# A selective state-space loop on one core: where the softplus mask lies, when the rows of C and x are projected, and when the step product is made

## The reference

```python
zxbcdt = hidden_states @ W_in.T
z, x, Bm, Cm, dtl = jnp.split(zxbcdt, splits, axis=-1)
delta = jax.nn.softplus(dtl @ W_dt.T + b_dt + b_dt)
x = repeat(x); x = jax.nn.silu(causal_conv4(x, conv_w) + conv_b)
def step(state, inp):                       # over 64 positions
    dA = jnp.exp(dlt[..., None] * A_g)      # 16 states a channel
    du = (dlt * u)
    state = dA * state + du[..., None] * Bs[:, :, None, :]
    y = jnp.einsum('bgdn,bgn->bgd', state, Cs)
    return (state, y)
y = ys + x * D_param
y = y * jax.nn.silu(z)
return y @ W_out.T
```

## Time and profile before

| what | value |
|---|---|
| median of three runs | 927.2 us |
| the profiled execution's own time | 926.82 us |
| span from its first to its last instruction | 924.9 us |
| state-space loop, first scan to end of the last | 41.5 to 273.8 us |
| DVE busy over the span | 548.1 us (59%) |
| ACT busy | 434.1 us (47%) |
| POOL busy | 302.3 us (33%) |
| PE busy | 818.7 us (89%) |

### The profile page before, as it was taken

The page is one execution under the profiler, slowest core; times in us unless marked ns, Lnnn a source line. Parts: engine busy times, 40 slices in busy tenths (PEclk is TensorE's granted clock), DMA queues, the critical chain, the costliest instruction groups (busy, mean ns, idle before and its releaser), DMA issues.

```text
span 924.9 us, 12509 instructions
## 1 busy us (share of the span) xinstructions
PE 818.7 (89%) x5082; PEld 501.8 (54%) x5082; DVE 548.1 (59%) x666; ACT 434.1 (47%) x650; POOL 302.3 (33%) x147
## 2 busy tenths in 40 slices
PE   6687797977999889999999899997989799989976
PEld 2232333322445456566666676666677566667754
DVE  3799989899994232333433452437872534464686
ACT  3764666635524555555545312233554222232475
POOL 0089999899870000000001010102009990000000
PEclk9889999899999999999999999998989999999999
DMA  9666666776994100000000031415000000000001
GB/s 301 176 172 172 185 166 172 181 182 181 249 264 157 47 1 1 1 1 1 1 1 25 27 103 57 176 44 226 2 3 1 1 1 1 1 1 1 1 1 46
DMA packets 26377, 77.02 MB, mean 83 GB/s; under 512 B 3569, under 2 KB 10481, under 8 KB 25073
## 3 DMA queue, kind: packets, MB, share of 16 engines
q1 hardware_dynamic: 25552, 74.13, 27.8%
q0 software_dynamic: 768, 2.10, 0.6%
HBM read 68.75 MB, written 7.08 MB: 82 GB/s over the span
## 4 chain that ended last, share of the span: by engine, by line
PE 54%; DVE 13%; DMA 11%; ACT 10%; POOL 6%; issue 5%; SPq 0%; POOLq 0%; DVEq 0%; ACTq 0%
PE ps L1268 11%; PE ps L1184 9%; DMA region_b<-m_rows 5%; DMA region_c<-m_rows 4%; PE ps L1231 4%; PE ps L1367 4%; PE ps L1393 4%; POOL region_c L464 3%; PE ps L1256 3%; PE ps L1189 2%; POOL region_b L464 2%; DVE region_c L1827 2%; PE ps L1073 2%; PE ps L1025 2%; PE ps L1158 2%
## 5 line engine op out<-in xcount | busy, mean ns | idle before, releaser
L464 POOL TENSOR_TENSOR region_c<-region_c,region_b 128x1024 f32<-128x1024 f32 x42 | 101.1, 2415 | 51.6 <-DMA region_b<-m_rows 45.5
L1073 PE MATMUL ps<-region_c,ident 128*128 128x512 f32 x168 | 90.7, 669 | 18.9 <-POOL region_c L464 12.1
L1827 DVE TENSOR_TENSOR_SCAN region_c<-region_c,ps 128x1024 f32<-128x1024 f32 x43 | 97.8, 2283 | 2.0 <-ACT ps L635 0.8
L485 POOL DMA_INDIRECT f_in<-xn,f_row x8 | 8.0, 996 | 275.3 <-DVE f_row L1938 273.5
L1268 PE MATMUL ps<-region_c 128*128 128x256 f32 x384 | 90.4, 381 | 0.1
L1268 PEld LDWEIGHTS ps<-region_c 128*128 128x128 f32 x384 | 72.2, 190 | 24.8 <-issue 16.3
L1904 DVE COPY region_b<-ps 128x512 f32<-128x512 f32 x32 | 21.6, 689 | 84.9 <-PE ps L1242 84.8
L1822 DVE TENSOR_TENSOR ps<-ps,region_c 128x1024 f32<-128x1024 f32 x52 | 63.2, 1215 | 8.7 <-PE ps L1061 8.5
L1073 PEld LDWEIGHTS ps<-region_c,ident 128*128 128x128 f32 x168 | 33.7, 209 | 58.5 <-issue 34.5
L1184 PE MATMUL ps<-xnT,region_a 128*128 128x512 f32 x128 | 61.5, 602 | 0.8 <-ACT region_c L703 0.8
L1184 PE MATMUL ps<-xnT,region_c 128*128 128x512 f32 x128 | 58.6, 594 | 0.7 <-ACT region_c L731 0.7
(11 more groups left out here) (246 smaller groups left out, 1640.8 us busy)
## 6 DMA issues: line engine op xcount, KB each, us to landing
region_b<-m_rows SPq DMA_DIRECT2D x43, 512.0 KB, 5.1
region_c<-m_rows SPq DMA_DIRECT2D x21, 512.0 KB, 4.9
xn<-m_brows SPq DMA_DIRECT2D x12, 512.0 KB, 4.4
region_a<-in_x_wo SPq DMA_DIRECT2D x2, 2048.0 KB, 11.5
m_rows<-region_b SPq DMA_DIRECT2D x4, 512.0 KB, 5.7
region_a<-in_x_wq SPq DMA_DIRECT2D x8, 256.0 KB, 7.2
region_b<-in_f_fc SPq DMA_DIRECT2D x1, 2048.0 KB, 7.9
region_b<-in_f_proj SPq DMA_DIRECT2D x1, 2048.0 KB, 13.2
```

Of the source, the lines that this page charges most:

```text
L464: pool.tensor_tensor(m_hc[u % 3], m_h[u % 3], m_cb[u % 3], ALU.mult).then_inc(sem("m_hc"), 1)
L1073: last = pe.matmul(ps[:, 4 + c, :], ident[:, :], m_hc[u % 3][:, c * HALF:c * HALF + HALF], start=(n == 0), stop=(n == DST - 1))
L1827: dve.tensor_tensor_scan(m_h[u % 3], m_da[u % 3].rearrange("p b t -> p (b t)"), inputs(u), 0.0, ALU.mult, ALU.add).then_inc(sem("m_scan"), 1)
```

## The change

1. The mask of the selection is written to PSUM pair 6, the pair into which the projections of C, x, z and the later convolutions go, and no longer to SBUF. So it has to lie between the C rows (and x rows) and the convolution: the convolution moves from n = 11 to n = 12 on PE and waits for the selection (`m_sel`), its copy on ACT from n = 12 to n = 13.
2. The C rows are projected at n = 2 and 3, not 3 and 4 (the first half ahead of `add_state`), and copied by ACT at n = 4, not 6. x is projected at n = 5 and 6, not 7 and 8, and copied at n = 7 and 8, not 9 and 10. The mask follows at n = 8, not 7.
3. The step product has a buffer for each block: `m_du` is a list, with the context's `ctxT` as block 1's buffer and the C rows' `m_rowsT` as block 3's. POOL makes it one step sooner, ahead of the state product of n = 13, directly behind the sum that gives delta. The load of `ctxT` moves from the start of the program to step 50.
4. On ACT the decay of a block's first step is issued ahead of the Silu `channels` of the same block, and not behind the two Silus.

The diff, whole but for its context:

```diff
-        m_du = view("C", 56, [TOK])
+        m_du = [view("C", 56, [TOK]), ctxT[:, :], view("C", 56, [TOK]), m_rowsT]
 # SP
-            load(ctxT[:, :], io["ctxT"], "ld_x0")
...
                     if n == 2:
                         sp.wait_ge(sem("m_delta"), NK)
                         sp.wait_ge(sem("m_u"), NK)
+                        sp.wait_ge(sem("m_pd"), len(SHARED) * (NK - 2))
+                        sp.wait_ge(sem("m_dbu"), own_products(DST * (NK - 2) - 1))
+                        load(ctxT[:, :], io["ctxT"], "ld_x0")
 # POOL
             def step_inputs(k):
                 pool.wait_ge(sem("m_u"), k + 1)
                 pool.wait_ge(sem("m_delta"), k + 1)
-                pool.wait_ge(sem("m_pd"), len(SHARED) * k)
-                pool.wait_ge(sem("m_dbu"), own_products(DST * k - 1))
-                pool.tensor_tensor(m_du, m_delta[k % 2].rearrange("p b t -> p (b t)"), m_u[:, k, :], ALU.mult)\
+                if k == 2:
+                    pool.wait_ge(sem("m_pd"), len(SHARED))
+                    pool.wait_ge(sem("m_dbu"), own_products(DST - 1))
+                if k == 3:
+                    pool.wait_ge(sem("st_rows"), 16 * NK)
+                pool.tensor_tensor(m_du[k], m_delta[k % 2].rearrange("p b t -> p (b t)"), m_u[:, k, :], ALU.mult)\
                     .then_inc(sem("m_du"), 1)
...
-                if n == DST - 2 and k < NK - 1:
+                if n == DST - 3 and k < NK - 1:
                     step_inputs(k + 1)
 # ACT
             def step_below(k):
-                act.activation(m_below, m_e, ACT.Relu, scale=-1.0, bias=thr_col).then_inc(sem("m_below"), 1)
+                act.wait_ge(sem("m_cT"), k + 1)
+                if k == 2:
+                    act.wait_ge(sem("m_xs"), 2)
+                act.activation(pair(6), m_e, ACT.Relu, scale=-1.0, bias=thr_col).then_inc(sem("m_below"), 1)
...
-            for u in range(NK * DST):
+            def decay(u):
                 k, n = u // DST, u % DST
                 if n == 0:
                     act.wait_ge(sem("m_delta"), k + 1)
...
+            for u in range(NK * DST):
+                k, n = u // DST, u % DST
+                if n or not k:
+                    decay(u)
...
-                    if n == 6:
+                    if n == 4:
                         c_rows(k + 1)
-                    if n == 7:
+                    if n in (7, 8) and k == 1:
+                        lags(1, (2 * n - 14, 2 * n - 13))
+                    if n == 8:
                         step_below(k + 1)
-                    if n in (9, 10) and k == 1:
-                        lags(1, (2 * n - 18, 2 * n - 17))
-                    if n == 12:
+                    if n == 13:
                         convolved(k + 1)
                     if n == DST - 1:
+                        decay(u + 1)
                         channels(k + 1)
 # PE
+                if n == 2 and k < NK - 1:
+                    pe.wait_ge(sem("m_ax"), k + 2)
+                    columns("C", k + 1, (0,))
                 if u >= 2:
                     add_state(u - 2)
...
-                    if n in (3, 4):
-                        pe.wait_ge(sem("m_ax"), k + 2)
-                        columns("C", k + 1, (n - 3,))
-                    if n in (7, 8) and k == 1:
+                    if n == 3:
+                        columns("C", k + 1, (1,))
+                    if n in (5, 6) and k == 1:
                         pe.wait_ge(sem("m_cT"), 3)
-                        columns("x", 1, (n - 7,))
-                    if n == 11:
-                        if k != 1:
-                            pe.wait_ge(sem("m_cT"), k + 2)
+                        columns("x", 1, (n - 5,))
+                    if n == 12:
+                        pe.wait_ge(sem("m_sel"), k + 1)
                         convolve(k + 1)
 # DVE: the selection reads pair(6), the products m_du[k]
-                dve.copy_predicated(m_ln, m_below.bitcast(mybir.dt.uint32), m_poly).then_inc(sem("m_sel"), 1)
+                dve.copy_predicated(m_ln, pair(6).bitcast(mybir.dt.uint32), m_poly).then_inc(sem("m_sel"), 1)
```

6 lines of the change are left out of this document (3 added, 3 removed).

## The result

The changed kernel takes 941.95 us (median of four runs, 940.29 to 943.13), the kernel before on the same chip 929.36 (924.82 to 933.08): ratio 1.0142, 95% interval 1.0107 to 1.0177. It is slower by 1.4%; the forecast of 930.3, range to 938, missed it. The profiled execution took 942.39 us with a span of 940.5.

A forecast was written before the change was run, and what follows sets the result against it. VectorE and GpSimd share the bound, GpSimd's chain setting the boundaries. Along GpSimd, -1.1, +1.7, +0.3 and +2.2 gave +3.1 us: 926.8 to 929.9, plus 0.4 for the median, 930.3; own range 926 to 936, widened 924 to 938.

The forecast's parts named there:

- The selection: Mask in PSUM, blocks 0 to 2: each selection 1.35 us in place of 3.37, freeing 2.0 of VectorE and 1.1 of GpSimd.
- 3 x 1.1 of my reading: Three selections: each frees 1.1 us of GpSimd, the only part that counts on the step product's path.
- The boundary up to scan 16: End of block 0: GpSimd idles 3.5 us before the step product; sum to scan 16 8.3 us against 6.1, +2.2.
- I keep half of GpSimd's waits in such a block: Blocks 1 and 2, with C rows sooner: of 3.7 and 4.3 us lost, 1.9 and 2.2 stay.
- In block 3 nothing is prepared, and all is passed on: Last block, scan 48 onward: the accumulated delay passes through with no further loss or gain, +0.
- C rows sooner: Block starts: a C half fills TensorE's idle 3.31 us, removing most of the waits at steps 21 and 22.
- x sooner: Block 1, scan 25: VectorE stalls 2.8 us for the shared input's copy; GpSimd sees about 1.1.
- Context load and convolution: Later ctxT load: 0 to 2.2 us once, taken as 0; convolution behind the selection: cover enough, no cost.
- The cold restart: Rival at the boundaries: TensorE at 1.2 GHz through two additions and a dt half, 3.4 us each, 940.5; chance 0.09.
- GpSimd's waits vanish: Rival, blocks 1 and 2: GpSimd, late from the boundary, finds each scan done; 55.4 + 3.5 each, 925.1; chance 0.22.
- The drain: ScalarE's table switches at the boundaries: about 1.38 us extra each, 4.1 in all by the page; left out, following the trace.

## Why the prediction was wrong

**The selection: right.** 1.31 us against 1.35 forecast, no stretched state product. The sum of block 0 ended 0.5 us sooner (92.95 against 93.48), not 1.1, and scan 0 had come 0.4 sooner by itself; with the mask alone it ended 2.5 us sooner with scan 0 1.0 sooner, so what the selection gives the sum differs between executions. By itself the mask is worth 4 us (0.9956), a little more than the 3 x 1.1 of my reading.

**The boundary up to scan 16: right in mechanism and size.** Gap 3.62 (forecast 3.5), sum to scan 16 101.36 - 92.95 = 8.4 us at all three boundaries (forecast 8.3, before 6.1). The experiments show its origin, the Silu behind a decay that waits for the sum: with the decay behind the Silus the gap is 1.1. That each boundary costs the loop 2.2 is in line with the 6.4 us left once the two late rows are gone, but not shown block by block.

**The failed step is what stands behind scan 16.** "I keep half of GpSimd's waits in such a block", 1.9 and 2.2 us, and "In block 3 nothing is prepared, and all is passed on". Along GpSimd's chain, forecast and measured:

| stretch | forecast | measured |
|---|---|---|
| block 1, sum to sum | 61.9 | 65.2 |
| block 2, sum to sum | 61.1 | 63.75 |
| last sum to scan 48 | 8.3 | 8.4 |
| scan 48 to scan 63, against before | +0 | +4.1 |

These are 3.3 + 2.65 + 0.1 + 4.1, with the 0.6 of block 0 10.8 us; the rest of the program was 1.7 us longer (655.1 us behind the start of scan 63, before 653.4), no more than it differs among the kernels timed here (652.0 to 658.3). Together they are the 12.5 us between the span that the sum gave, 928.0, and the 940.5 measured. Of the 24 instructions' 55.4 us the measured blocks hold 55.8, so the instructions were right and the waits were not. GpSimd stood idle for 9.4 us of block 1 and 8.0 of block 2; without the gap of 3.6 that is 5.8 and 4.4, where I had 3.0 (1.9 and the 1.1 for x) and 2.2. Of these, 2.31 and 2.48 are one wait each, that of the state product of step 16 or 32; the rest, 3.5 and 1.9, is near the forecast. So halving the waits of the old kernel was about right (with mask and C sooner alone GpSimd stood idle for 2.3 us in each of the two blocks, before 3.4 and 4.0). What the sum lacks is a new wait behind each boundary, 2.31, 2.48 and 2.50 us, 7.3 in all (for the third the profile names TensorE, but the row of C landed at 237.16, 0.13 ahead of the state product).

The cause is the one resource that I followed too short. I saw that the late state product of step 13 frees a scan buffer. The same instruction also releases the C row of step 16 on SyncE's queue, 5.4 us later than before, with a landing of 6.4 us behind it, and TensorE's addition. Both come behind scan 16 and hold step 16's state product and step 17's product for 2.31 us each. Without them scans 16 to 20 are back at 14.2 us and scans 48 to 63 at 51.2. My text had no sentence on SyncE's queue at the boundary at all.

These two explain 6.7 us of the miss. Of the other 5.8, 1.7 lie behind the loop and 0.6 ahead of the first boundary, where the executions differ anyway; the rest is in small terms of blocks 1 to 3 that no single run prices.

**C rows sooner: right where TensorE comes out of its idle time at full clock** (product of step 21 waits 0.58 instead of 1.75; ratio 0.9912 against 0.9956 for the mask alone, intervals that just touch), and nothing in the executions where it doesn't (3.13). In the changed kernel it waited 1.43. **x sooner:** the stall of scan 25 was 2.96 us (forecast 2.8). Forecast to cost 1.1, it costs 1.6 in block 1 of a kernel without the gaps, by one profile of each, and nothing measurable in one with them. **Context load and convolution: right at about nothing**; the load at the start again gave 941.4, and scans 48 to 63 took 53.9 us in place of 55.1.

**The rivals.** The cold restart was the one on the slow side, with 940.5 near the measured value, but not for its reason. It was to cost 10.2 us by lasting over two additions and a dt half; it lasted over the first four matmuls and the row of B (3.78 and 1.06 us, then 2.19 and 1.88), and taking it away alone changed the time by nothing measurable. It is one of two late things that are worth 6.7 us together. The prediction held the low clock's duration for what decides; it named no wait of GpSimd on a row of C in any rival. That GpSimd's waits vanish was the wrong sign: they grew. The drain that the Trainium skill adds to a table switch (ScalarE: Activation LUTs, What ACT_TABLE_LOAD costs) was rightly left out of the sum: in the gap the load follows the decay by 0.01 us and the Silu follows the load by 0.02.

## What to carry to other kernels

When a step slips on an engine that executes in order, list everything that its completion releases, the DMA queues' buffers too, and follow each to its first user; a load that was prefetched with little slack (here 0.7 us) turns a delay of its release into a wait further down (here 5.4 us into 2.3). An instruction put ahead of another costs more than its own move if the other was the cover of a wait: here two moves cost 4 and 5 us apart and 13 together. On GpSimd, busy for some 56 of 60 us, gaps of 3.4, 3.9 and 10.9 us in all went with losses of 5, 4 and 13, so put a wait on a producer behind everything that other engines still need from that list.

## What the runs showed of the hardware

- **TensorE's clock after short idleness has no one outcome.** After 6.10, 5.12 and 6.09 us of idleness the restart was at 1.2 GHz at all three boundaries (3.78 us for four matmuls, full level 1.88). In the five other kernels that kept this idle time (5.1 to 6.1 us, fifteen boundaries) it was 3.42 to 3.78. After 2.21 us it was 3.60 in one execution and 1.98 in another, with nearly the same work ahead; after 1.77 or 1.78 us it was 1.98 or 2.87 to 3.56, in two blocks of one and the same execution too. Runs of the kernels that sit at this edge spread over several us (918.68 to 930.88), and the mean granted clock goes with them (0.972 at the fastest, 0.956 at the slowest). The four runs of the changed kernel, cold at every boundary of its profile, lie within 3 us; the link is argued from these figures, not tested.
- Eight matmuls of 512 columns took 3.70 us after 2.25 us of idleness, and the addition behind them 1.98.
- A copy_predicated whose mask lies in PSUM took 1.31 us beside a busy GpSimd. With the mask in SBUF it took what was left of GpSimd's running instruction and some 1.2 more: 3.40 in the earlier trace rows, where 2.17 were left, and 1.46 in block 1 of the changed kernel with the mask in SBUF, where 0.24 were left (it started at 149.16, GpSimd's instruction ended at 149.40). GpSimd paid 1.1 us either way: the next state product took 3.48 and 3.45 in place of 2.37.
- Of two row broadcasts (512 KB each) asked for 0.36 us apart, the first landed after 4.2 us and the second after 5.8 at the boundary before. In the changed kernel, with a third asked for 1.9 us behind the second, it was 4.3 and 6.4, and 6.6 for the third.
